# A graph and expert layer on one core: set-up transfers by lane, small loads on GpSimd, and a later wait for DRAM copies

## The chip, the cores and the metric

The kernel runs on one core of a Trainium2 chip. The metric is the device time of one execution in microseconds (us), taken as the median of the runs; lower is better. Engines are named by their work: TensorE (PE), VectorE (DVE), ScalarE (ACT), GpSimd (POOL), and SyncE (SP), which does no arithmetic and whose queue issues DMA transfers. ACT and POOL have DMA queues of their own.

## The reference

One layer over 6250 nodes with 256 features and 200,000 edges sorted by their destination. What matters of it:

```python
edge_index = jnp.stack([src, dst])
xn = _layernorm(x, axis=-1)
x = x + _L0_gnn_ref(xn, edge_index, W, att_src, att_dst, bias) + _L0_mix_ref(xn[None], Wqkv, bqkv, Wproj, bproj, temperature)[0]
x = x + _L0_ffn_ref(_layernorm(x, axis=-1)[None], gate_w, gate_b, w1, b1, w2, b2, gamma, beta)[0]
```

The graph part gathers a projected row for each edge's source, weighs it by a softmax over the edges of its destination, and sums by destination. The mix part is an attention whose keys and values are first summed over all nodes. The last part sends each node to two of 16 experts.

## The kernel before

The work is cut into stages, each a block with a program per engine. At the end of a block all engines meet, and none starts the next block before the last has come. The stages are set-up, projection (50 tiles of 128 nodes), gather (the edges), routing, experts, and the final norm.

Edges are taken in chunks of 496 (CHUNK); 403 chunks are full and one holds the rest of 112. The gather stage wants, for each chunk, a list of source numbers that lies lane by lane: `src_lists` in DRAM is 128 lanes by 408 chunks by 4 places. Lanes 0 to 119 hold four edges of a chunk, lanes 120 to 127 two, and their other places must hold a harmless number. The lists are written by DMA from `src`, DRAM to DRAM. The lists of the first 384 chunks are written beside the tiles of the projection stage, eight chunks at a time (lines 871 and 873); the tail, chunks 384 to 403, is written in set-up.

In set-up the SP queue issues, in this order: the first destinations and the padded destinations, the node features x into `resid` (lines 343 and 345), the pads of `src_lists` (line 348, and line 351 once for each of eight lanes), the tail of the lists for lanes 0 to 119 (line 354), a wait for the pads, the tail for lanes 120 to 127 (line 357), the last chunk (line 359), six tiles of zero rows (line 362), eight loads of one temperature each into `t_col` (line 366) and one of `bq_col` (line 367), `b1_cols` (line 369), and four tiles of `dst_bc` (line 372). It then waits until all DRAM copies but the pads have landed (`scratch_out`). VectorE meanwhile takes the statistics of x, and near its end waits for the small loads (line 484) before it scales `t_col` (line 485) and turns `meet`. GpSimd issues three bias loads (line 389) and, once VectorE has computed where each block of nodes begins, four gathers of destination rows, `d_rows` (line 394).

At the head of the projection stage VectorE clears the last 32 lanes of `rows_g` (line 751), clears four PSUM banks (line 753) and sets constants; ScalarE's first copy of `p_row` (line 643) waits for the last of them. At the end of that stage SP waits for the lists written beside the tiles and fetches the first ones for the gather stage.

Of the kernel before, what the change touches and what calls it, by code (L numbers as in the profile page):

```python
# [19 lines left out]
P = 128  # L20
# [117 lines left out]
def gps_layer(nc, x, src, dst, gnn_W, att_src, att_dst, gnn_bias, Wqkv, bqkv, Wproj, bproj, temperature,  # L138
# [12 lines left out]
    with top:  # L151
# [57 lines left out]
        rows_g = sb("rows_g", [P, R, TC, ROW], ctx=early)  # L209
        idx_in = [sem(f"idx_in{i}", early) for i in range(2)]  # L210
        gather_opened = sem("gather_opened", early)
        gathered = [sem(f"gathered{i}", early) for i in range(R)]

        def gather(pool, q, j):
# [29 lines left out]
        with ExitStack() as c:  # L244
# [50 lines left out]
            x_rest_in = sem("x_rest_in", c)  # L295
            w_in = sem("w_in", c)
            b_in = sem("b_in", c)
            t_in = sem("t_in", c)
            att_zeroed = sem("att_zeroed", c)
            att_in = sem("att_in", c)  # L300
            pads_set = sem("pads_set", c)
            scratch_out = sem("scratch_out", c)
            lists_padded = sem("lists_padded", c)
            ident_ready = sem("ident_ready", c)
            turned = sem("turned", c)
            copied = sem("copied", c)
# [18 lines left out]
            @block.sync  # L325
            def _(sp):
                full = E // CHUNK
                rest = E - full * CHUNK
                even = full - full % 16
                for lo, hi in ((0, even), (even, full)):  # L330
                    sp.dma_start(fd[:, lo:hi], dst[lo * CHUNK:hi * CHUNK].rearrange("(c b) -> c b", b=CHUNK)[:, 0:1].rearrange("c a -> a c"),
                                 allow_slow_non_contiguous=True).then_inc(first_in, 16)
                sp.dma_start(fd[:, full:full + 1], dst[full * CHUNK:full * CHUNK + 1].unsqueeze(0)).then_inc(first_in, 16)
                for lo, hi in ((0, even), (even, full)):
                    sp.dma_start(dst_pad[lo:hi, :], dst[lo * CHUNK:hi * CHUNK].rearrange("(a b) -> a b", b=CHUNK)).then_inc(dst_padded, 16)
                sp.dma_start(dst_pad[full:full + 1, 0:rest], dst[full * CHUNK:E].unsqueeze(0)).then_inc(dst_padded, 16)
                sp.wait_ge(pads_set, 3)
                sp.dma_start(dst_pad[full:full + 1, rest:CHUNK], pad_i[0:1, 0:CHUNK - rest]).then_inc(dst_padded, 16)
                sp.dma_start(dst_pad[full + 1:CHUNKS, :], pad_i[0:CHUNKS - full - 1, :]).then_inc(dst_padded, 16)
                sp.wait_ge(x_zeroed, 1)  # L340
                for q in range(4):
                    n = NFULL // 4
                    sp.dma_start(resid[:, q * n:(q + 1) * n, :],
                                 x[q * n * P:(q + 1) * n * P, :].rearrange("(t p) f -> p t f", p=P)).then_inc(x_in[q], 16)
                sp.dma_start(resid[0:NREST, NFULL, :], x[NFULL * P:N, :]).then_inc(x_rest_in, 16)
                u4 = TILES_PER_CHUNK
                last = rest // u4
                sp.dma_start(src_lists[:, full:CHUNKS, :], pad_s[:, 0:(CHUNKS - full) * u4].rearrange("p (a u) -> p a u", u=u4)).then_inc(lists_padded, 16)
                lo = LIST_TILES * LIST_CHUNKS
                for p in range(LANES, P):  # L350
                    sp.dma_start(src_lists[p:p + 1, 0:full, :].rearrange("p a u -> p (a u)").rearrange("p (a b) -> (p a) b", a=u4),
                                 pad_s[0:u4, 0:full]).then_inc(lists_padded, 16)
                tail = src[lo * CHUNK:full * CHUNK].rearrange("(a b) -> a b", b=CHUNK)
                sp.dma_start(src_lists[0:LANES, lo:full, :].rearrange("p a u -> a p u"),
                             tail[:, 0:BASE].rearrange("a (p u) -> a p u", u=u4)).then_inc(scratch_out, 16)
                sp.wait_ge(lists_padded, (1 + EXTRA) * 16)
                sp.dma_start(src_lists[LANES:P, lo:full, 0:FULL_TILES].rearrange("p a u -> a p u"),
                             tail[:, BASE:CHUNK].rearrange("a (p u) -> a p u", u=FULL_TILES)).then_inc(scratch_out, 16)
                sp.dma_start(src_lists[0:last, full:full + 1, :].rearrange("p a u -> p (a u)"),
                             src[full * CHUNK:E].rearrange("(p u) -> p u", u=u4)).then_inc(scratch_out, 16)  # L360
                for t in range(T, TQ):
                    sp.dma_start(xn_turned[t * P:(t + 1) * P, :], zrow[:]).then_inc(scratch_out, 16)
                heads = temperature.rearrange("a h b c -> (a h b c)")
                for h in range(H):
                    p0 = (h % HALF) * C
                    sp.dma_start(t_col[p0:p0 + C, h // HALF:h // HALF + 1], heads[h:h + 1].unsqueeze(0).broadcast_to([C, 1])).then_inc(t_in, 16)
                sp.dma_start(bq_col[:], bqkv[0:D].rearrange("(g p) -> p g", p=P), allow_slow_non_contiguous=True).then_inc(t_in, 16)
                sp.wait_ge(copied, len(turns) + 1)
                sp.dma_start(b1_cols.rearrange("e p c -> p e c"), b1_t[:].rearrange("p (e c) -> p e c", e=NEXP)).then_inc(scratch_out, 16)
                for g in range(G4):  # L370
                    sp.wait_ge(rows_taken, g + 1)
                    sp.dma_start(dst_bc[g * P:(g + 1) * P, :], d_bf[g][:]).then_inc(scratch_out, 16)
                sp.wait_ge(scratch_out, (3 + TQ - T + G4 + 1) * 16)

            @block.gpsimd
            def _(pool):
# [11 lines left out]
                for ap, vec, n in ((b_kv, bqkv[D:3 * D], 2 * D), (b_proj, bproj, D), (b_gnn, gnn_bias, D)):  # L388
                    pool.dma_start(ap[:], bcast_rows(vec, n)).then_inc(b_in, 16)
                pool.iota(ci[:], [[1, CHUNKS]], base=0, channel_multiplier=0).then_inc(chunk_nr, 1)  # L390
                pool.wait_ge(dst_padded, 5 * 16)
                pool.wait_ge(b_ready, 1)
                for g in range(G4):
# [3 lines left out]
            def _(dve):  # L397
# [82 lines left out]
                dve.reciprocal(rstd[:], rstd[:])  # L480
                dve.drain()
                dve.scalar_tensor_tensor(out=nmr[:], in0=mv[:, :, 0], scalar=-1.0, in1=rstd[:], op0=ALU.mult, op1=ALU.mult)
                dve.wait_ge(b_in, 3 * 16)
                dve.wait_ge(t_in, (H + 1) * 16)
                dve.tensor_scalar(t_col[:], t_col[:], SCALE * SCALE, None, ALU.mult)
                dve.wait_ge(meet_turned, 1)
                dve.tensor_copy(meet[:, 0:FCH, :], p_meet[:, 0:FCH * C].rearrange("p (m i) -> p m i", i=C))
# [77 lines left out]
        with ExitStack() as c:  # L565
# [182 lines left out]
            @block.vector  # L748
            def _(dve):
                dve.memset(zeros[:], 0.0)  # L750
                dve.memset(rows_g[P - C:P].rearrange("p r u f -> p (r u f)"), 0.0)
                for bank in p_main + p_tg:
                    z = dve.memset(bank[:], 0.0)
                z.then_inc(zeroed, 1)
                dve.tensor_scalar(vmask[:], valid[:], 1.0 / N, None, ALU.mult)
                for s in range(2):
                    dve.memset(k1[s][:], 1.0)
# [103 lines left out]
            def _(sp):  # L861
# [15 lines left out]
                for t in range(LIST_TILES, T):  # L877
                    body(t, t % 2)
                sp.wait_ge(lists_out, 2 * LIST_TILES * 16)
                fetch_lists(sp, 0, 0)  # L880
                fetch_lists(sp, R, 1)
                for s in range(2):
# [1149 lines left out]
```

## Time and profile before

| | us |
|---|---|
| median of 3 runs | 3235.82 |
| the runs | 3235.3, 3235.82, 3238.56 |
| the profiled execution | 3240.07 |
| its span | 3238.3 |
| set-up, in the profile | 0 to 78.3 |
| first to last gather of the gather stage | 403.7 to 2478.2 |

The profile is one execution. Its times count from the start of the span; a row of the timeline gives the start, the duration, the engine, the line of the kernel, what is written and read, and in brackets how long the engine was idle before and what released it. SPq, ACTq and POOLq are the queues that issue DMAs: the duration of such a row is that of the issue, not of the transfer. PEclk is the granted clock of TensorE, 1.00 for 2.4 GHz.

### The profile page before, as it was taken

What the parts mean: (1) busy time and instruction counts of PE and PEld (TensorE: products, weight loads), DVE (VectorE), ACT (ScalarE), POOL (GpSimd) and SP (SyncE); (2) the same over time, 40 slices, a digit from 0 to 9 for tenths busy, and PEclk for the clock granted to TensorE, in tenths of its full rate; (3) what the DMA queues carried; (4) which work ended last, traced back from release to release, by engine and by line L of the source; (5) the groups of instructions that cost most, each with busy time, mean ns of one, the idle gap of its engine ahead of it and who ended that gap; (6) DMA issues with size and microseconds to landing.
All of it is one profiled execution on the core that took longest, in us unless ns stands there. A gap on an engine that the chain in (4) does not pass through costs nothing. (4 is left out here: it accounts for less than half of the span.)

```text
span 3238.3 us, 54302 instructions
## 1 busy us (share of the span) xinstructions
PE 2620.3 (81%) x12344; PEld 1709.4 (53%) x12344; DVE 2165.1 (67%) x5140; ACT 1459.4 (45%) x3473; POOL 2079.2 (64%) x2145
## 2 busy tenths in 40 slices
PE   2999978888887888888787888888755438999996
PEld 1455444444544455454444454554444437888884
DVE  5888877767777676777777676777767844333335
ACT  1444465545555555555464555555433221222226
POOL 0577777777777777777777777777775572222224
PEclk9999989989999898999899989889986559999998
DMA  5222244444545444454444444444443156777867
GB/s 146 44 46 45 41 141 136 141 137 130 142 130 142 131 139 134 136 142 130 142 131 136 136 136 136 136 134 132 134 132 90 58 183 188 232 233 233 233 203 244
DMA packets 303697, 454.51 MB, mean 140 GB/s; under 512 B 121983, under 2 KB 198072, under 8 KB 303442
## 3 DMA queue, kind: packets, MB, share of 16 engines
q0 software_dynamic: 88848, 243.01, 26.7%
q1 hardware_dynamic: 186434, 135.90, 15.7%
q10 hardware_dynamic: 28176, 72.95, 6.9%
q8 instruction: 84, 1.38, 0.2%
q14 instruction: 155, 1.27, 0.1%
HBM read 396.32 MB, written 56.94 MB: 140 GB/s over the span
## 5 line engine op out<-in xcount | busy, mean ns | idle before, releaser
L219 POOL DMA_INDIRECT rows_g<-node_rows,idx x1616 | 1577.9, 976 | 497.8 <-issue 461.1
L1211 PE MATMUL p_m<-msg,sel 128*128 128x264 f32 x3616 | 1043.6, 438 | 254.3 <-DVE msg L1179 207.7
L1211 PEld LDWEIGHTS p_m<-msg,sel 128*128 128x128 f32 x3616 | 727.3, 212 | 390.6 <-issue 272.0
L1179 DVE TENSOR_TENSOR msg<-rows_g,p_w 128x1024 f32<-128x1024 f32 x452 | 550.6, 1218 | 44.8 <-ACT p_w L1077 43.7
L1077 ACT ACTIVATE p_w<-lg 128x32 f32<-128x32 f32 x452 | 91.0, 201 | 785.1 <-DVE lg L1172 783.8
L1863 POOL DMA_INDIRECT moe<-ysb,token x128 | 124.0, 969 | 366.3 <-DVE ysb L1852 343.3
L1168 DVE TENSOR_TENSOR lg<-rows_g,ends 128x32 f32<-128x32 f32 x452 | 87.2, 193 | 406.7 <-SPq L1011 306.0
L1032 ACT ACTIVATE sel_t<-apart,ones 128x512 bf16<-128x512 bf16 x455 | 328.4, 722 | 32.1 <-issue 0.7
L1101 DVE TENSOR_TENSOR sel<-p_w,dst_t 128x512 f32<-128x512 f32 x453 | 312.1, 689 | 26.4 <-issue 9.3
L1029 ACT ACTIVATE apart<-dst_all,iota_neg 128x512 bf16<-128x512 bf16 x455 | 321.6, 707 | 0.0
L1201 PEld LDWEIGHTS p_sp<-adm_parts,sel_t 128*128 128x128 bf16 x1816 | 94.5, 99 | 382.1 <-issue 374.2
L1055 ACT ACTIVATE qfeat<-p_scr 128x512 f32<-128x512 f32 x442 | 239.4, 588 | 116.9 <-PE p_scr L1234 111.2
L1818 ACT ACTIVATE ht<-e_ph,ba 128x256 f32<-128x256 f32 x256 | 100.3, 474 | 418.2 <-PE e_ph L1788 418.2
L562 POOL TENSOR_TENSOR acc<-kk 128x512 f32<-128x512 f32 x150 | 167.7, 1147 | 156.5 <-DVE kk L796 156.5
L1234 PE MATMUL p_scr<-q_t,sel_sum 32*128 32x512 f32 x832 | 248.8, 653 | 5.2 <-DVE q_gram L1130 5.2
L1788 PE MATMUL e_ph<-xst,wa 128*128 128x256 f32 x1024 | 233.3, 382 | 4.2 <-DMA bb<-in_L_ffn_b_dram 2.5
L1797 PE MATMUL e_py<-wb,ht 128*128 128x256 f32 x1024 | 231.5, 380 | 0.0
L1788 PEld LDWEIGHTS e_ph<-xst,wa 128*128 128x128 f32 x1024 | 195.7, 192 | 31.8 <-issue 5.5
L1201 PE MATMUL p_sp<-adm_parts,sel_t 128*128 x1816 | 125.1, 188 | 107.5 <-DVE lg L1172 97.7
L1827 DVE COPY xst<-e_px 128x512 f32<-128x512 f32 x64 | 44.3, 692 | 238.1 <-PE e_px L1778 238.1
L1797 PEld LDWEIGHTS e_py<-wb,ht 128*128 128x128 f32 x1024 | 190.1, 191 | 22.8
L1110 DVE TENSOR_TENSOR acc<-acc,p_m 128x264 f32 x452 | 194.1, 430 | 6.1 <-PE p_m L1211 3.5
(331 smaller groups left out, 3358.1 us busy)
## 6 DMA issues: line engine op xcount, KB each, us to landing
dst_all<-dst_bc ACTq DMA_DIRECT2D x115, 512.0 KB, 4.2
wa<-in_L_ffn_w_dram SPq DMA_DIRECT2D x64, 512.0 KB, 4.8
wb<-in_L_ffn_w_dram SPq DMA_DIRECT2D x64, 512.0 KB, 5.3
rows_g<-node_rows,idx POOLq DMA_INDIRECT x1616
xs<-slot_x SPq DMA_DIRECT2D x64, 258.0 KB, 2.9
ya<-moe SPq DMA_DIRECT2D x48, 256.0 KB, 4.4
bb<-in_L_ffn_b_dram SPq DMA_DIRECT2D x64, 128.0 KB, 5.6
qs<-xn_turned ACTq DMA_DIRECT2D x13, 512.0 KB
```

The costliest lines, as they stand in the source:

```text
L219: pool.indirect_dma_start(rows_g[0:n, j, u, :], None, node_rows, bass.IndirectOffsetOnAxis(ap=idx[q][0:n, j, u:u + 1], axis=0)).then_inc(g ...
L1029: act.activation(apart[j % 2][:], dst_all[q][:, j, :], ACT.Square, bias=iota_neg[:])
L1032: act.activation(sel_t[j][:], apart[j % 2][:], ACT.Relu, bias=ones[:, 0:1], scale=-1.0).then_inc(sel_t_ready, 1)
L1055: act.activation(feat[slot(name)][:], bank(name)[:], ACT.Square).then_inc(act_freed, 1)
L1101: dve.tensor_tensor(sel[j][:], p_w[:, P:2 * P].unsqueeze(1).broadcast_to([P, TC, P]), d.unsqueeze(2).broadcast_to([P, TC, P]), ALU.is_equa ...
L1110: dve.tensor_tensor(a, a, p_m[j % 2][:, 0:ROW], ALU.add).then_inc(acc_added, 1)
L1179: dve.tensor_tensor(m4, g3[:, :, 0:D].rearrange("p u (h e) -> p u h e", h=H), p_w[:, 0:TC * H].rearrange("p (u h) -> p u h", u=TC).unsquee ...
L1201: mm = pe.matmul(p_e(j)[:, u * 6 * H:(u + 1) * 6 * H], sel_t[j][:, u * P:(u + 1) * P], adm_parts[:, bass.ds(b, 1), :, :].rearrange("p a r ...
L1211: mm = pe.matmul(p_m[j % 2][:, 0:ROW], sel[j][:, u, :], msg[j % 2][:, u, :], start=(u == 0), stop=(u == TC - 1))
L1234: pe.matmul(bank(name)[:], sel_sum[rows, m * P:(m + 1) * P], q_t[g][rows, :], start=True, stop=True).then_inc(act_filled, 1)
L1788: mm = pe.matmul(p_h[s % 2][:, m * SLOT_ROWS:(m + 1) * SLOT_ROWS], wa[s][:, k, m * P:(m + 1) * P], xst[s % 2][:, k, :], start=(k == 0), st ...
L1797: mm = pe.matmul(p_y[s % 2][:, a * D:(a + 1) * D], ht[s % 2][:, k, a * P:(a + 1) * P], wb[s][:, k, :], start=(k == 0), stop=(k == KF - 1))
```

## The change

Five edits, all of set-up and of its two neighbours in time:

- The eight pad transfers, one per spare lane, become four that each cover all eight lanes.
- The tail of the lists is described lane first (`p a u`) on both sides, in place of chunk first (`a p u`). The bytes are the same.
- The eight loads of `t_col` and the load of `bq_col` move from SP's queue to GpSimd's, behind the bias loads, and count on the same semaphore `b_in`.
- The three tail transfers count on a new semaphore, `tail_out`. SP waits for it at the end of the projection stage, before the first lists are fetched, and no longer at the end of set-up.
- The fill of `rows_g` moves behind the PSUM fills and covers only the places that a partial gather leaves open (two of four).

```diff
-                for p in range(LANES, P):
-                    sp.dma_start(src_lists[p:p + 1, 0:full, :].rearrange("p a u -> p (a u)").rearrange("p (a b) -> (p a) b", a=u4),
-                                 pad_s[0:u4, 0:full]).then_inc(lists_padded, 16)
+                spare_lanes = src_lists[LANES:P, 0:full, :].rearrange("p a u -> p (a u)")
+                for q in range(u4):
+                    sp.dma_start(spare_lanes[:, q * full:(q + 1) * full], pad_s[0:EXTRA, 0:full]).then_inc(lists_padded, 16)
                 tail = src[lo * CHUNK:full * CHUNK].rearrange("(a b) -> a b", b=CHUNK)
-                sp.dma_start(src_lists[0:LANES, lo:full, :].rearrange("p a u -> a p u"),
-                             tail[:, 0:BASE].rearrange("a (p u) -> a p u", u=u4)).then_inc(scratch_out, 16)
-                sp.wait_ge(lists_padded, (1 + EXTRA) * 16)
-                sp.dma_start(src_lists[LANES:P, lo:full, 0:FULL_TILES].rearrange("p a u -> a p u"),
-                             tail[:, BASE:CHUNK].rearrange("a (p u) -> a p u", u=FULL_TILES)).then_inc(scratch_out, 16)
+                sp.dma_start(src_lists[0:LANES, lo:full, :], tail[:, 0:BASE].rearrange("a (p u) -> p a u", u=u4)).then_inc(tail_out, 16)
+                sp.wait_ge(lists_padded, (1 + u4) * 16)
+                sp.dma_start(src_lists[LANES:P, lo:full, 0:FULL_TILES], tail[:, BASE:CHUNK].rearrange("a (p u) -> p a u", u=FULL_TILES)).then_inc(tail_out, 16)
                 sp.dma_start(src_lists[0:last, full:full + 1, :].rearrange("p a u -> p (a u)"),
-                             src[full * CHUNK:E].rearrange("(p u) -> p u", u=u4)).then_inc(scratch_out, 16)
+                             src[full * CHUNK:E].rearrange("(p u) -> p u", u=u4)).then_inc(tail_out, 16)
...
-                heads = temperature.rearrange("a h b c -> (a h b c)")
-                for h in range(H):
-                    p0 = (h % HALF) * C
-                    sp.dma_start(t_col[p0:p0 + C, h // HALF:h // HALF + 1], heads[h:h + 1].unsqueeze(0).broadcast_to([C, 1])).then_inc(t_in, 16)
-                sp.dma_start(bq_col[:], bqkv[0:D].rearrange("(g p) -> p g", p=P), allow_slow_non_contiguous=True).then_inc(t_in, 16)
...
-                sp.wait_ge(scratch_out, (3 + TQ - T + G4 + 1) * 16)
+                sp.wait_ge(scratch_out, (TQ - T + G4 + 1) * 16)
...
+                heads = temperature.rearrange("a h b c -> (a h b c)")
+                for h in range(H):
+                    p0 = (h % HALF) * C
+                    pool.dma_start(t_col[p0:p0 + C, h // HALF:h // HALF + 1], heads[h:h + 1].unsqueeze(0).broadcast_to([C, 1])).then_inc(b_in, 16)
+                pool.dma_start(bq_col[:], bqkv[0:D].rearrange("(g p) -> p g", p=P), allow_slow_non_contiguous=True).then_inc(b_in, 16)
...
-                dve.wait_ge(b_in, 3 * 16)
-                dve.wait_ge(t_in, (H + 1) * 16)
+                dve.wait_ge(b_in, (3 + H + 1) * 16)
...
-                dve.memset(rows_g[P - C:P].rearrange("p r u f -> p (r u f)"), 0.0)
                 for bank in p_main + p_tg:
                     z = dve.memset(bank[:], 0.0)
                 z.then_inc(zeroed, 1)
+                dve.memset(rows_g[P - C:P, :, FULL_TILES:, :], 0.0)
...
                 sp.wait_ge(lists_out, 2 * LIST_TILES * 16)
+                sp.wait_ge(tail_out, 3 * 16)
                 fetch_lists(sp, 0, 0)
```

## Rows read from the trace of the kernel before

**Rows 1.** Timeline of SP's queue in set-up: start, issue time, line, transfer, count.

```profile
30.63 2.90 SPq L351 DMA_DIRECT2D src_lists<-pad_s  x8
33.58 0.75 SPq L354 DMA_DIRECT2D src_lists<-in_src_dram  x1
38.53 23.14 SPq L357 DMA_DIRECT2D src_lists<-in_src_dram  x1
61.72 1.73 SPq L359 DMA_DIRECT2D src_lists<-in_src_dram  x1
63.49 2.97 SPq L362 DMA_DIRECT2D xn_turned<-zrow  x6
66.50 3.70 SPq L366 DMA_DIRECT2D t_col<-n_L_mix_temperature_dram  x8
70.25 0.43 SPq L367 DMA_DIRECT2D bq_col<-in_L_mix_bqkv_dram  x1
70.73 0.46 SPq L369 DMA_DIRECT2D b_cols<-b_t  x1
71.23 2.43 SPq L372 DMA_DIRECT2D dst_bc<-d_bf  x4
```

**Rows 2.** Waits of SP's queue: for what, us in total, times, longest.

```profile
SPq L244 <- DMA dst_bc<-d_bf: 4.2, 1, 4.2
```

**Rows 3.** Timeline of VectorE's and ScalarE's rows at set-up's end.

```profile
45.33 0.21 DVE L482 SCALAR_TENSOR_TENSOR nmr<-mv,rstd 128x50 f32<-128x50 f32 x1
...
72.51 0.17 DVE L485 TENSOR_SCALAR t_col<-t_col 128x2 f32<-128x2 f32 x1 [26.97 <-DMA bq_col<-in_L_mix_bqkv_dram]
...
73.06 0.17 DVE L489 TENSOR_SCALAR meet<-meet 32x32 f32<-32x32 f32 x1
78.28 1.09 ACT L630 ACTIVATE xn<-resid,nmr,rstd 128x256 f32<-128x256 f32 x2 [33.53 <-PEq L244]
```

**Rows 4.** Windows: length, busy PE, PEld, DVE, ACT, POOL, PEclk, DMA share, GB/s.

```profile
44.00:50.00 6.00, 0.00 (x0) 0.00 (x0) 1.08 (x5) 0.24 (x1) 0.00 (x0) 1.00 0.12 1
...
66.00:68.00 2.00, 0.00 (x0) 0.00 (x0) 0.00 (x0) 0.00 (x0) 0.00 (x0) 1.00 0.63 202
...
72.00:74.00 2.00, 0.00 (x0) 0.00 (x0) 0.63 (x3) 0.00 (x0) 0.00 (x0) 1.00 1.08 103
```

**Rows 5.** One line's instructions: count, duration min/median/max in ns, first and last start.

```profile
L871 SPq DMA_DIRECT2D src_lists<-in_src_dram x48: 702/754/826, 88.6 to 382.7; - x48
```

**Rows 6.** Timeline of GpSimd in set-up, and VectorE's last use of d_rows.

```profile
3.69 0.56 POOL L389 DMA_DIRECT2D b_gnn<-in_L_gnn_bias_dram  x1
...
22.98 1.02 POOL L394 DMA_INDIRECT d_rows<-dst_pad,cidx  x1 [18.29 <-DVE b L451]
...
33.34 0.63 DVE L471 TENSOR_SCALAR d_bf<-d_rows,b 128x480 bf16<-128x480 int32 x1
```

**Rows 7.** Timeline of the projection stage: VectorE's fill, and TensorE after gaps.

```profile
79.84 3.58 DVE L751 MEMSET rows_g<- 32x4224 f32 x1 [0.92 <-issue]
...
89.25 1.46 PE L711 MATMUL p_row<-w_cat,xt 128*128 128x272 f32 x4 [4.52 <-ACT xt L637]
...
90.50 3.35 PE L711 MATMUL p_kv<-w_cat,xt 128*128 128x512 f32 x4
...
378.32 1.88 PE L711 MATMUL p_kv<-w_cat,xt 128*128 128x512 f32 x4
...
398.60 1.92 PE L684 MATMUL p_main<-acc,vm 128*32 128x512 f32 x16 [2.52 <-DVE acc L562]
```

**Rows 8.** Windows of the projection stage: TensorE alone, then all engines.

```profile
91.00:92.00 1.00, 1.00 (x2) 0.50 0.25 71
...
320.00:340.00 20.00, 19.90 (x112) 11.02 (x111) 17.33 (x42) 10.14 (x33) 14.59 (x17) 1.00 0.24 49
```

**Rows 9.** The gathers of line 219: durations in ns, and what ended idle time.

```profile
L219 POOL DMA_INDIRECT rows_g<-node_rows,idx x1616: 947/987/1487, 403.7 to 2478.2; - x180
...
  DVE msg L1179: 33.3, 101
```

More of the change, by code:

```diff
@@ L211, in gps_layer @@
         gather_opened = sem("gather_opened", early)
+        tail_out = sem("tail_out", early)
         gathered = [sem(f"gathered{i}", early) for i in range(R)]
@@ L297, in gps_layer @@
             b_in = sem("b_in", c)
-            t_in = sem("t_in", c)
             att_zeroed = sem("att_zeroed", c)
@@ L301, in gps_layer @@
             pads_set = sem("pads_set", c)
+            lists_padded = sem("lists_padded", c)
             scratch_out = sem("scratch_out", c)
-            lists_padded = sem("lists_padded", c)
             ident_ready = sem("ident_ready", c)
```

## The prediction

> **What bounds the kernel now.** I read the profile from the edit outwards. The slices of the page show two long stages that the change does not enter: the gather stage, and the expert stage behind it. In the gather stage GpSimd issues 1616 gathers in 2074.5 us, one each 1.28 us: 0.99 for the issue itself and 0.3 to the next one. Only 33.3 us of it is a wait for VectorE [rows 9]. Its length is set by the number of gathers, so a gain in set-up moves this stage forward and does not shorten it.
>
> The change lies in set-up (0 to 78.3 us) and at the head of the projection stage. The timeline of the SP queue shows that one issue, line 357, holds the queue from 38.53 to 61.67 [rows 1]. The windows show why: from 44 to 50 us the DMA engines are at a share of 0.12 and move 1 GB/s [rows 4]; this is the first of five windows that are alike, up to 64 us. The transfer of line 354, issued at 33.58, has 19 chunks as its outermost count and 19 x 120 = 2280 pieces of 16 bytes; it crawls on a corner of the DMA engines, and the next issue waits until its pieces are through. Everything behind it is late: eight loads of t_col and the load of bq_col are issued at 66.50 and 70.25, and VectorE, ready at 45.54, waits for them 26.97 us [rows 1, 3]. ScalarE sits from 44.8 until the next block opens at 78.28 [rows 3]. Yet VectorE's own last step ends at 73.23; what closes the block is SP, which issues dst_bc until 73.66 and waits 4.2 us for the landing, to 77.87 [rows 1 to 3]. The barrier takes the other 0.4.
>
> **The change part by part.**
>
> Pads (line 351). Eight issues of 2.90 us in all [rows 1] become four: 1.45 less at the front. It buys nothing alone, because SP then stands until 38.53 for the landing of the pads (the wait ahead of line 357) [rows 1], which lie behind the x loads. I keep 38.53. Bounds: 36.5 if the landing follows fewer pieces and the queue behind x (at 36 to 38 us almost nothing moved), 40.4 if the new tail, now on the same engines as all pads, costs them its own 1.9 us (next part).
>
> Tail of the lists (lines 354, 357, 359). Now lane by lane: outermost count 120, with the same pieces read from src. One corner of the engines took from about 34 to 64 us for some 2400 pieces, 12.4 ns a piece; spread over 15 to 16 engines that is 1.9 us. The nearest row of a spread transfer is b1_cols: 2048 pieces of 16 bytes with 128 outermost, gone together with the first of dst_bc in the windows 72 to 74, where the share is 1.08 [rows 4]. The lists of the later tiles, 960 pieces with 8 outermost, are issued in a median of 754 ns and never hold SP [rows 5]. So line 357 costs 0.75 in place of 23.14 and line 359 0.75 in place of 1.73 [rows 1, 5]; bounds 0.3 each (a pad's issue) and 1.7. The Trainium skill, "DMA: Bandwidth & Descriptors", section on why a DMA increments its semaphore by 16, says that a transfer runs on the largest number of engines up to 16 that divides the outermost counts of both sides: by it 19 gives one engine and 120 gives fifteen. No row here shows a transfer with 120 outermost.
>
> Small loads. The nine leave SP, 3.70 + 0.43 us with the steps between them 4.2 [rows 1], and go to GpSimd behind its iota, at 4.69. GpSimd's own loads take 0.56 each in the last case [rows 6] and up to 0.74; nine are 5.0 to 6.6 us, so it is free by about 11.5. It waits there for VectorE until 22.98 [rows 6], a cover of 11 us. If the cover were gone, the four gathers of d_rows behind them would start late; the last is used at 33.34 without slack [rows 6], and VectorE would slip by as much. VectorE's one merged wait for b_in at 45.5 finds all landed. Here a page speaks against the edit. The Trainium skill, "SBUF — State Buffer", on the trap that VectorE blocks DMAs issued from GpSimd, says that these descriptors can't be written while a VectorE instruction in a two-port mode runs. The trace does not bear it out at this place: GpSimd issued b_gnn in 0.56 us at 3.69 to 4.25, beside VectorE's back-to-back fills [rows 6].
>
> New end of the block. SP: 38.53, then 0.75 + 0.75 for lines 357 and 359, 2.97 for the zero rows, 0.46 for b1_cols, 2.43 for dst_bc, and five steps of 0.05: 46.1 [rows 1]. The landing of dst_bc takes 4.2 more [rows 2]. The 768 KB of zero rows ran at about 200 GB/s [rows 4], some 1.3 us past their own issue; in the kernel before, the nine loads gave them time to drain, now b1_cols follows at once. I add 1.0 (bounds 0 and 1.3), which makes 51.3, and the barrier of 0.4: the next block opens at 51.7, against 78.28. Gain 26.6. The next to be late is VectorE: 45.54 and its last three steps of 0.75, done at 46.3, 5.0 us under SP. The wait for tail_out now stands before the first list fetch, at about 365 us; it costs nothing, its transfers are long down, and what is queued behind it on SP (the list fetches) loses nothing.
>
> Bounds of this term: earliest 51.7 - 2.0 (pads) - 0.9 (two issues) - 1.0 (backlog) = 47.8; latest 51.7 + 1.9 + 1.9 + 0.3 = 55.8. The gain is 22.5 to 30.5.
>
> Fill of rows_g. In the projection stage VectorE fills 4224 columns in 3.58 us [rows 7] before the PSUM fills and the constants that ScalarE's first copy waits for. It now fills 2112 after the PSUM fills: at the same rate 1.79, so 1.79 less on that path; the first tile was waiting for it, since TensorE's first projection was done by 84.5. Gain 1.8, with no cover.
>
> TensorE's clock. In this gap TensorE idled 4.52 us before 89.25 [rows 7], its granted clock then fell to 0.50 (1.2 of 2.4 GHz) [rows 8], and the four matmuls of p_kv took 3.35 us [rows 7] against 1.88 in a later tile [rows 7]. With the fill shortened the gap is 4.52 - 1.79 = 2.73. A gap of 2.52 us later in the stage kept the upper level: the sixteen matmuls behind it ran in the usual 1.92 [rows 7]. 2.73 is nearer to that than to 4.52, so I take the clock as kept: 3.35 - 1.88, gain 1.5. The bounds are 0 and 1.5. From there the stage is full of TensorE (19.90 of 20 us [rows 8]), so an early first tile stays early.
>
> **The sum.** 26.6 + 1.8 + 1.5 = 29.9 us. The profiled execution took 3240.07 (span 3238.3), so its like would be 3210.2; the median of the three runs is 4.25 lower, and I apply the same difference: 3235.82 - 29.9 = 3205.9.
>
> **The rivals.**
>
> A: the tail does not spread (0.06). If the pieces still go through one corner, line 357 stalls for its 23.14 again. Then only the nine loads leave SP, 4.2, plus 1.8: 3235.8 - 6.0 = 3229.8. For it: the bytes and the pieces are the same. Against it: the lists with 8 outermost and b1_cols with 128 both run without a stall [rows 4, 5].
>
> B: another cover is used up (0.06). Either reading 16-byte pieces at a stride of a chunk costs some five times the 12.4 ns, so that 152 pieces per engine last 9.4 us in place of 1.9 and hold zero rows, b1_cols and dst_bc, all on the same engines (7.5 later); or the small loads take over 1.9 us each on GpSimd and push d_rows and VectorE past the 5.0 us of room. Priced by the first: 3213.4. Speaking for it: 16-byte reads at a stride are seen in no row. Against: the writes of before were scattered in the same way at 12.4 ns. The skill's rule on the shared port takes the second road: if not one of the nine loads got through before VectorE's b128 was ready at 22.1, they would end near 28, d_rows would be 5.0 late and VectorE level with SP. By the issue times of this trace that is 3205.9 still; it decides only from there on, and 0.01 of B's chance is for it.
>
> C: slower (0.03). In the gather stage VectorE holds GpSimd 101 times, 33.3 us in all [rows 9]; VectorE stands there behind TensorE, whose clock moves between 0.78 and 1.00 from one 50 us window to the next. An earlier start deals these phases anew. The hold would have to grow from 33.3 to over 63 us for the result to be worse than before; at 70 it would be 3242. For it: the profiled run was 4.25 over the median of the others. Against it: three runs lay within 3.3 us, so a growth of 30 is far out of what this stage does by itself.
>
> **How the numbers follow.** The main case has 0.85; its own range is gains from 22.5 + 1.8 + 0 - 2 (spread of runs) = 22.3 to 30.5 + 1.8 + 1.5 + 2 = 35.8, that is 3200.0 to 3213.5. B's price is just inside; this is the range for 8 in 10. A measurement of this kernel can tell about 0.2% (6.5 us) from no change. Faster by more: the main case and B, 0.91. Within: A, whose 6.0 is just under, 0.06. Slower: C, 0.03.
>
> **What would show it.** Line 357's issue under 2 us and zero rows issued from about 40; the DMA share of 0.12 gone; VectorE's wait for t_col gone and its last step of set-up near 46.3; the next block open at 47.8 to 55.8 with SP's wait for dst_bc as the last one; the first copy of p_row 1.8 us sooner after the opening; the second tile's four matmuls of p_kv in 1.9 (kept) or 3.35 (lost); the gather stage, first to last gather, at 2074.5 us as before within 2. A stalled line 357 would make A true, and d_rows used later than 33.3 would point to B. The forecast is wrong if the first gather does not move by about 30 from 403.65, or if the later stages give part of it back.

## The result, and the profile after

| | before | changed |
|---|---|---|
| median, first set of runs, us | 3235.61 (3235.3 to 3238.56, 4 runs) | 3211.41 (3209.23 to 3213.59, 4 runs) |
| ratio, with its 95% interval | | 0.9923 (0.9911 to 0.9934) |
| median, second set | 3237.72 (3234.68 to 3240.88, 9 runs) | 3217.47 (3210.66 to 3219.61, 5 runs) |
| ratio, second set | | 0.9936 (0.9922 to 0.9949) |
| the profiled execution | 3240.07 | 3213.59 |
| next block opens after set-up | 78.28 | 54.51 |
| first gather | 403.7 | 376.3 |

The change is faster by 24.2 us in the first set and by 20.3 in the second. The forecast was 3205.9, a gain of 29.9, with a range from 3200.0 to 3213.5: the first median lies inside, 5.5 above the forecast. The second, 3217.47, lies 4.0 above the end of the range, and its gain of 20.3 is below the smallest gain of the range, 22.3.

SP's queue in the changed kernel, by its timeline (start, issue time, line, transfer, count), answers to [rows 1]:

```profile
31.36 2.06 SPq L352 DMA_DIRECT2D src_lists<-pad_s  x4
33.47 0.97 SPq L354 DMA_DIRECT2D src_lists<-in_src_dram  x1
42.59 0.73 SPq L356 DMA_DIRECT2D src_lists<-in_src_dram  x1
43.36 0.85 SPq L357 DMA_DIRECT2D src_lists<-in_src_dram  x1
44.25 2.96 SPq L360 DMA_DIRECT2D xn_turned<-zrow  x6
47.25 0.45 SPq L362 DMA_DIRECT2D b_cols<-b_t  x1
47.75 2.49 SPq L365 DMA_DIRECT2D dst_bc<-d_bf  x4
```

The stall of 23.14 us is gone: the second tail transfer (now line 356) is issued in 0.73. But it starts at 42.59 and not at 38.53. SP's waits, which answer to [rows 2], name the reason:

```profile
SPq L356 <- DMA src_lists<-pad_s: 8.1, 1, 8.1
SPq L245 <- DMA dst_bc<-d_bf: 3.8, 1, 3.8
```

The rest of set-up, by the timeline of GpSimd, VectorE and ScalarE [rows 3, 6]:

```profile
4.64 4.02 POOL L387 DMA_DIRECT2D t_col<-n_L_mix_temperature_dram  x8
...
8.65 0.75 POOL L388 DMA_DIRECT2D bq_col<-in_L_mix_bqkv_dram  x1
...
23.01 1.04 POOL L392 DMA_INDIRECT d_rows<-dst_pad,cidx  x1 [13.61 <-DVE b L449]
...
45.48 0.16 DVE L482 TENSOR_SCALAR t_col<-t_col 128x2 f32<-128x2 f32 x1
...
46.02 0.17 DVE L486 TENSOR_SCALAR meet<-meet 32x32 f32<-32x32 f32 x1
...
54.51 1.09 ACT L627 ACTIVATE xn<-resid,nmr,rstd 128x256 f32<-128x256 f32 x2 [9.74 <-PEq L245]
```

VectorE's idle time ahead of t_col is gone, the small loads are off GpSimd by 9.40, and SP alone closes the block. The head of the projection stage answers to [rows 7]:

```profile
57.86 1.82 DVE L751 MEMSET rows_g<- 32x2112 f32 x1 [0.49 <-issue]
...
58.29 3.43 PE L708 MATMUL p_kv<-w_cat,xt 128*128 128x512 f32 x4
...
61.82 0.38 ACT L640 COPY row<-p_row 128x264 f32<-128x264 f32 x1 [5.55 <-PE p_kv L708]
...
63.29 1.18 PE L708 MATMUL p_row<-w_cat,xt 128*128 128x272 f32 x4 [1.35 <-ACT xt L634]
...
64.31 1.88 PE L708 MATMUL p_kv<-w_cat,xt 128*128 128x512 f32 x4
```

And the gathers, which answer to [rows 9]:

```profile
L220 POOL DMA_INDIRECT rows_g<-node_rows,idx x1616: 952/987/1507, 376.3 to 2453.2; - x180
...
  DVE msg L1177: 31.1, 94
```

### The profile page after: what moved, and what is told of

The parts are those of the page before. It is cut to its first block and busy times, and to the rows that moved or that the text cites. A ratio compares the mean times of both kernels' runs of the same rounds, so it can differ in the third digit from the quotient of the medians.

```text
span 3211.8 us, 54298 instructions
## 1 busy us (share of the span) xinstructions
PE 2620.5 (82%) x12344; PEld 1708.0 (53%) x12344; DVE 2164.7 (67%) x5140; ACT 1460.0 (45%) x3473; POOL 2085.8 (65%) x2154
## 5 line engine op out<-in xcount | busy, mean ns | idle before, releaser
L1027 ACT ACTIVATE apart<-dst_all,iota_neg 128x512 bf16<-128x512 bf16 x455 | 321.7, 707 | 0.0
```

Of the source, the lines that this page charges most:

```text
L1027: act.activation(apart[j % 2][:], dst_all[q][:, j, :], ACT.Square, bias=iota_neg[:])
```

## The experiments

The theory after the result: the gain is the end of the stall of line 357, and what is missing of it was lost at the wait for the pads, which the tail, now spread over the engines right behind them, holds up (theory T). Its rival is that the four wide pad transfers land late by themselves (P). Of the tail's slowness there are two accounts, strided reads (S) and any spread small pieces (Q); of TensorE, theory K ties its clock to the gap that the fill shortens. The labels in brackets are those that the expectations use. Twelve runs were made, of ten kernels besides the changed one, which ran again, as did best1; u_ kernels undo a part of the changed kernel, o_ kernels make one part alone in the kernel before. Most have one profiled execution beside one of the kernel before, so they are read by places in the trace and not by their time: single executions took 3209.6 us (u_pads) to 3218.7 (iso) where the tail is spread, 3233.0 with the small loads only and 3231.8 with the fill only, beside 3237.7 to 3241.7 for the kernel before. A table of the places comes at the end of this section.

### The tail behind the pads' wait (u_order)

```diff
-                sp.dma_start(src_lists[0:LANES, lo:full, :], tail[:, 0:BASE].rearrange("a (p u) -> p a u", u=u4)).then_inc(tail_out, 16)
                 sp.wait_ge(lists_padded, (1 + u4) * 16)
+                sp.dma_start(src_lists[0:LANES, lo:full, :], tail[:, 0:BASE].rearrange("a (p u) -> p a u", u=u4)).then_inc(tail_out, 16)
```

> The changed kernel, but the big tail transfer (lane first, 2280 pieces) is issued behind the wait for the pads and not ahead of it. Theory T (the tail, spread over the engines and issued right behind the pads, holds up the pads' landing, which took SP to 42.59 us): the wait for the pads ends at 38.5 or before, and the tail, now alone on the engines, shows its own length in the DMA windows. Rival P (the four wide pad transfers land late by themselves): the wait still ends near 42.6. If the tail's pieces cost 12.4 ns each on one engine and spread over 15, its stretch is 2 us long; if a read at a stride costs five times as much, 8 us.

SP's queue by the timeline:

```profile
38.41 0.96 SPq L355 DMA_DIRECT2D src_lists<-in_src_dram  x1
...
45.12 10.61 SPq L365 DMA_DIRECT2D dst_bc<-d_bf  x4
```

The wait ended at 38.41: theory T holds and P falls. The gain was not kept: the four issues of dst_bc took 10.61 us in place of 2.49, one of them alone 9.1, and the next block opened at 57.70, 3.2 us later than in the changed kernel. The spread tail costs whoever is queued around it, the pads ahead of it or dst_bc behind it.

### The narrow pads back (u_pads)

```diff
-                spare_lanes = src_lists[LANES:P, 0:full, :].rearrange("p a u -> p (a u)")
-                for q in range(u4):
-                    sp.dma_start(spare_lanes[:, q * full:(q + 1) * full], pad_s[0:EXTRA, 0:full]).then_inc(lists_padded, 16)
+                for p in range(LANES, P):
+                    sp.dma_start(src_lists[p:p + 1, 0:full, :].rearrange("p a u -> p (a u)").rearrange("p (a b) -> (p a) b", a=u4),
+                                 pad_s[0:u4, 0:full]).then_inc(lists_padded, 16)
...
-                sp.wait_ge(lists_padded, (1 + u4) * 16)
+                sp.wait_ge(lists_padded, (1 + EXTRA) * 16)
```

> The changed kernel with the eight narrow pad transfers of before in place of the four wide ones. Theory T: the wait for the pads still ends near 42.6. Rival P: it ends near 38.5 as before the change, and the next block opens 4 us sooner than 54.5.

The wait ended at 43.03 and the block opened at 55.00. With eight narrow transfers the landing is as late as with four wide ones, so the pads' form is not the cause. The opening is 0.5 us later than the changed kernel's, no more than two profiles of that kernel differ (54.51 and 55.04), so no gain of the pads' edit by itself is shown.

### The tail only (o_tail)

The two transfers of chunks 384 to 402 lane first in the kernel before, awaited in set-up as before, and nothing else.

> The kernel before with one part alone: the three tail transfers lane first (awaited in set-up as before, narrow pads, small loads on SP). If the corner of the engines was all of the stall: the issue of line 357 under 1 us, but the pads' wait ends near 42.6 by theory T (38.5 by P), then zero rows, nine loads (4.2 us), b1_cols, dst_bc; the next block opens near 78.3 - 22 + 4 = 58 to 60 by T, 54 to 56 by P. It would be worth some 18 to 20 of the 26.5 us that the profiled runs differ.

The second tail transfer on SP's queue, and ScalarE's first instruction of the next block:

```profile
44.74 0.72 SPq L356 DMA_DIRECT2D src_lists<-in_src_dram  x1
...
60.77 1.09 ACT L628 ACTIVATE xn<-resid,nmr,rstd 128x256 f32<-128x256 f32 x2 [16.00 <-PEq L244]
```

The block opened at 60.77, 17.5 us sooner than 78.28, with the wait for the pads ending at 44.74. This is by far the largest part of the gain; the opening is a little later than the 58 to 60 of T. The small loads alone give 3.6 (below), so the two parts together account for 21.1 of the 23.8 us by which the changed kernel opens sooner; of the other 2.7, 2.2 is the end of the pads' wait, 44.74 against 42.59, a place that differs by 1.4 between two profiles of the changed kernel itself. Here set-up still waited for the tail, and its last wait was put down to dst_bc, 3.8 us, as in the changed kernel: keeping the tail's wait in set-up cost nothing to be seen in this kernel.

### The tail by itself (iso)

All else of set-up first, then the big tail transfer with nothing beside it, then a wait for it alone:

```diff
-                sp.dma_start(src_lists[0:LANES, lo:full, :], tail[:, 0:BASE].rearrange("a (p u) -> p a u", u=u4)).then_inc(tail_out, 16)
...
                 sp.wait_ge(scratch_out, (TQ - T + G4 + 1) * 16)
+                sp.dma_start(src_lists[0:LANES, lo:full, :], tail[:, 0:BASE].rearrange("a (p u) -> p a u", u=u4)).then_inc(tail_out, 16)
+                sp.wait_ge(tail_out, 16)
...
```

The two small tail transfers stand behind that wait.

> The price in dispute by itself: the changed kernel with the big tail transfer (lane first) issued when everything else of set-up has landed, and SP waiting for it alone before it issues the two small ones and closes the block. Without the tail in the way the wait for the pads ends by 38.5 and dst_bc has landed near 48. Then issue to landing of the tail: 12.4 ns a piece on each of fifteen engines gives 1.9 us and some 2 us of landing, 4 in all; theory S (a read of 16 bytes at a stride of a chunk costs about 50 ns) gives 8 and 2, 10 in all.

SP's queue and its wait, then the windows (length, PEclk, DMA share, GB/s), the last two of them finer:

```profile
48.53 0.96 SPq L363 DMA_DIRECT2D src_lists<-in_src_dram  x1
60.42 0.73 SPq L365 DMA_DIRECT2D src_lists<-in_src_dram  x1
```

```profile
SPq L365 <- DMA src_lists<-in_src_dram: 10.9, 1, 10.9
```

```profile
48.00:50.00 2.00, 1.00 0.00 0
50.00:52.00 2.00, 1.00 0.46 13
52.00:54.00 2.00, 1.00 0.14 4
54.00:56.00 2.00, 1.00 0.04 1
56.00:58.00 2.00, 1.00 0.00 0
58.00:60.00 2.00, 1.00 0.00 0
...
54.25:54.50 0.25, 1.00 0.14 4
54.50:54.75 0.25, 1.00 0.00 0
```

From the start of the issue to the landing it takes 11.9 us. I had put 1.9 for the pieces and about 2 for landing. The first pieces show 1.7 us after the start of the issue, and the last are through by 54.5, some 4 us later, most of them in the first two; then for 5.9 us no transfer is recorded and the semaphore still does not come. The shares of the windows add up to 20.5 us of one engine's time (0.64 of 16 engines over 2 us), 9 ns for each of the 2280 pieces. This is an estimate. It is below 12.4, and below the 24 ns that the same reckoning gives for the confined pieces (0.12 of 16 engines over 30 us for some 2400): the price of a piece was not put too low. What the 1.9 us lacked is the time around the pieces. Theory S, a steady 8 us of slow pieces, is not seen either, although its total of 10 is the nearer one. Spread out, the tail went from some 28 us (an estimate: 2280 pieces at 12.4 ns) to 11.9, not to a fifteenth.

### The tail chunk first, in 16 and 3 chunks (split)

```diff
-                sp.dma_start(src_lists[0:LANES, lo:full, :], tail[:, 0:BASE].rearrange("a (p u) -> p a u", u=u4)).then_inc(tail_out, 16)
+                lists_t, chunks_t = src_lists[0:LANES].rearrange("p a u -> a p u"), tail[:, 0:BASE].rearrange("a (p u) -> a p u", u=u4)
+                for a0, a1 in ((0, 16), (16, full - lo)):
+                    sp.dma_start(lists_t[lo + a0:lo + a1], chunks_t[a0:a1]).then_inc(tail_out, 16)
...
-                sp.wait_ge(tail_out, 3 * 16)
+                sp.wait_ge(tail_out, 4 * 16)
```

> The changed kernel with the big tail chunk first as before, but in two transfers of 16 and 3 chunks: 16 and 3 are the outermost counts, the reads are whole rows of 1920 bytes, the writes 16 bytes each. Theory S (the strided reads are what is slow and holds up the pads): the wait for the pads ends near 39 and the next block opens near 51. Rival Q (any tail that is spread over the engines right behind the pads holds them up, by its scattered pieces): the wait still ends near 42.6. If the outermost count were not what spreads a transfer, line 357's stall of 23 us would be back.

The timeline shows the two issues together (line 356) and the end of the wait (line 358):

```profile
33.87 4.11 SPq L356 DMA_DIRECT2D src_lists<-in_src_dram  x2
41.95 0.72 SPq L358 DMA_DIRECT2D src_lists<-in_src_dram  x1
```

The stall of 23 us did not come back: the same chunk-first pieces, with 16 and 3 outermost in place of 19, flow, though the longer of the two issues took 3.42 us. That shows the outermost count to be what confined the transfer of before. The wait ended at 41.95, far from S's 39: whole-row reads did not free the pads, so the strided read is not what holds them up. Rival Q, that any spread tail right behind them does, is the nearer one. The block opened at 53.04.

### SP's queue turned round (best1, best1_r, and after_r beside it)

Zero rows, b1_cols and dst_bc first; the wait for the pads and the three tail transfers behind them:

```diff
-                sp.dma_start(src_lists[0:LANES, lo:full, :], tail[:, 0:BASE].rearrange("a (p u) -> p a u", u=u4)).then_inc(tail_out, 16)
-                sp.wait_ge(lists_padded, (1 + u4) * 16)
-                sp.dma_start(src_lists[LANES:P, lo:full, 0:FULL_TILES], tail[:, BASE:CHUNK].rearrange("a (p u) -> p a u", u=FULL_TILES)).then_inc(tail_out, 16)
-                sp.dma_start(src_lists[0:last, full:full + 1, :].rearrange("p a u -> p (a u)"),
-                             src[full * CHUNK:E].rearrange("(p u) -> p u", u=u4)).then_inc(tail_out, 16)
                 for t in range(T, TQ):
...
                     sp.dma_start(dst_bc[g * P:(g + 1) * P, :], d_bf[g][:]).then_inc(scratch_out, 16)
+                sp.wait_ge(lists_padded, (1 + u4) * 16)
+                sp.dma_start(src_lists[0:LANES, lo:full, :], tail[:, 0:BASE].rearrange("a (p u) -> p a u", u=u4)).then_inc(tail_out, 16)
+                sp.dma_start(src_lists[LANES:P, lo:full, 0:FULL_TILES], tail[:, BASE:CHUNK].rearrange("a (p u) -> p a u", u=FULL_TILES)).then_inc(tail_out, 16)
+                sp.dma_start(src_lists[0:last, full:full + 1, :].rearrange("p a u -> p (a u)"),
+                             src[full * CHUNK:E].rearrange("(p u) -> p u", u=u4)).then_inc(tail_out, 16)
                 sp.wait_ge(scratch_out, (TQ - T + G4 + 1) * 16)
```

> The changed kernel with the order of SP's queue turned round: zero rows, b1_cols and dst_bc ahead of the wait for the pads, all three tail transfers behind it; the block still closes on the landing of dst_bc and the rest. SP issues dst_bc from 37.4 to 39.9, it lands by 44 to 45, so VectorE's 46.3 closes the block and the next opens near 46.7, 7.8 us sooner than 54.5. If the tail, issued at about 40, slows dst_bc's landing, it opens at 50. The first copy of p_row then still waits for TensorE, 7.3 us after the opening, and the first gather comes near 368.5.

The block opened at 46.47 as expected, with VectorE as the last to come. The first gather came at 369.9 and not at 368.5, since TensorE's clock was lost once more (below), and the span ended at 3212.0, level with the changed kernel's 3211.8. Both kernels were timed again together:

> The changed kernel again, timed beside best1_r on one chip. If the gather stage's length (2071 to 2082 us in ten profiles, all of it in the length of the single issues) is a matter of the run, the gains of the set-up will show in the medians: about 3211. If it belongs to the kernel, this one keeps a gather stage of about 2077.

> The kernel of best1 again, with rounds. Its profile opened the projection stage 8.0 us sooner than the changed kernel and began the gathers 6.4 us sooner, but ended at the same time: 4.4 us went in the gather stage, 2.2 behind it. If that is chance (issues of 980 ns against 978 on average, over 1616), the median is 3205 to 3206, some 5 to 6 us under after_r. If an earlier start makes the gather stage longer, it is level with after_r within 2 us and its profile again has 2081 us from first to last gather.

The changed kernel's median was 3217.47, as in the table above. The turned-round one had 3206.74 (3203.02 to 3208.39, 4 runs), 0.9904 of the kernel before (0.9889 to 0.9919): 31.0 us faster than before and 10.7 faster than the changed kernel beside it. The runs of the two do not overlap, so the turned-round kernel is faster. Both expectations missed in size: the changed kernel was put at about 3211 and the difference at 5 to 6. The profiles show 8.4 us of the 10.7, at the opening and again at the first gather; where the rest lies they do not show, as each is of the fastest run of its kernel, and these two differ by 7.6. The loss of the clock in the first profile did not come again in the second. In that one the block opens at 46.67 and the first gather comes at 368.3:

```profile
34.00 2.79 SPq L355 DMA_DIRECT2D xn_turned<-zrow  x6
36.84 0.46 SPq L357 DMA_DIRECT2D b_cols<-b_t  x1
37.34 4.81 SPq L360 DMA_DIRECT2D dst_bc<-d_bf  x4
42.19 0.97 SPq L362 DMA_DIRECT2D src_lists<-in_src_dram  x1
```

The tail is now behind all that set-up waits for, and its landing falls into the projection stage. This kernel beats both the one before and the changed one.

### The same, with the big tail transfer still ahead (best2)

> As best1, but the big tail transfer stays right behind the pads, ahead of the zero rows. If its pieces share the rings with dst_bc (u_order: issue of dst_bc 10.6 us), b1_cols and dst_bc are slow and the block opens at 50 to 54; if only the waiting for the pads had mattered, it opens near 47 as best1.

Its issues ran into the tail: the zero rows took 6.5 us to issue in place of 2.8, dst_bc 9.2, and the block opened at 51.64. So it is not the wait for the pads alone that costs; the transfer itself must be behind dst_bc. Not all of the long issue is the tail's: in the first turned-round profile, with no tail ahead, one issue of dst_bc took 3.8 us, and here one took 7.8.

### The small loads only (o_loads)

> The kernel before with one part alone: the nine small loads on GpSimd's queue. Line 357 still holds SP for some 23 us. By the sum the next block opens 4.2 us sooner, at 74.1, and the first copy of p_row is 9.4 us behind it as before; if the loads had only given the zero rows time to drain, half a microsecond to one of that is lost again in the landing of dst_bc. GpSimd is free by 11.5 and d_rows is issued at 23.0 as before.

The block opened at 74.70: 3.6 us sooner, against 4.2 of the sum, and the wait for the pads ended 0.6 later than before (39.13). VectorE had nothing to wait for. d_rows was unharmed, as in the changed kernel.

### The fill of rows_g: undone, and alone (u_fill, o_fill)

```diff
+                dve.memset(rows_g[P - C:P].rearrange("p r u f -> p (r u f)"), 0.0)
                 for bank in p_main + p_tg:
                     z = dve.memset(bank[:], 0.0)
                 z.then_inc(zeroed, 1)
-                dve.memset(rows_g[P - C:P, :, FULL_TILES:, :], 0.0)
```

> The changed kernel with the fill of rows_g as before: all 4224 columns, ahead of the PSUM fills. Set-up unchanged: the block opens at 54.5. Theory K (the shorter gap of TensorE keeps its clock): the first copy of p_row comes 9.4 us after the opening in place of 7.3; TensorE idles some 3.5 us or more between the first two tiles, its clock is lost, and the second tile's four matmuls of p_kv take 3.4 us in place of 1.9; the first gather comes 3.6 to 3.9 us later than 376.3. Rival (the clock is not tied to this gap): 2.1 us later only, with p_kv at 1.9.

> The kernel before with one part alone: the fill of rows_g halved and behind the PSUM fills. The block opens at 78.3 as before. The first copy of p_row comes 2.1 to 2.3 us sooner after it. Theory K: TensorE's gap between the first two tiles falls from 4.5 to some 2.3 us, the clock stays, the second tile's four matmuls of p_kv take 1.9 in place of 3.35, and the first gather comes 3.7 to 4.0 us sooner than 403.65. If a gap of this length can still lose the clock (best1's of 2.09 did), it comes 2.2 us sooner only.

TensorE's timeline at the second tile, first with the fill undone, then with the fill alone changed in the kernel before:

```profile
67.05 2.18 PE L708 MATMUL p_row<-w_cat,xt 128*128 128x272 f32 x4 [3.92 <-ACT xt L634]
69.02 3.59 PE L708 MATMUL p_kv<-w_cat,xt 128*128 128x512 f32 x4
```

```profile
86.74 1.18 PE L711 MATMUL p_row<-w_cat,xt 128*128 128x272 f32 x4 [2.54 <-ACT xt L637]
87.76 1.88 PE L711 MATMUL p_kv<-w_cat,xt 128*128 128x512 f32 x4
```

With the fill undone the gap is 3.92 us, both groups of matmuls of the second tile run at the lower clock, and the first gather comes 326.4 us after the opening in place of 321.8. That is 4.6 and not the 3.6 to 3.9 expected, 1.0 of it because p_row too ran at the lower clock (2.18 against 1.18). With the fill alone the gap is 2.54, the clock stays, and it comes 321.7 after the opening in place of 325.4. What theory K expected came true in both directions; that the length of the gap alone does not decide is said below.

### All profiles side by side

"Opens" is the start of ScalarE's first instruction of the projection stage; p_kv is the time of the four matmuls of the second tile; all in us.

| kernel | pads' wait ends | opens | TensorE's gap | p_kv | opening to first gather | first to last gather |
|---|---|---|---|---|---|---|
| before | 38.53 | 78.28 | 4.52 | 3.35 | 325.4 | 2074.5 |
| changed | 42.59 | 54.51 | 1.35 | 1.88 | 321.8 | 2076.9 |
| changed, again | 43.97 | 55.04 | 1.33 | 1.88 | 321.7 | 2075.0 |
| tail behind the wait | 38.41 | 57.70 | 1.34 | 1.88 | 321.8 | 2076.8 |
| narrow pads back | 43.03 | 55.00 | 1.33 | 1.88 | 321.9 | 2074.5 |
| tail only | 44.74 | 60.77 | 3.92 | 3.59 | 326.4 | 2070.9 |
| tail by itself | 38.63 | 62.78 | 2.44 | 1.88 | 321.5 | 2075.8 |
| chunk first, 16 and 3 | 41.95 | 53.04 | 1.22 | 1.88 | 322.0 | 2081.6 |
| turned round | | 46.47 | 2.09 | 2.62 | 323.4 | 2081.3 |
| turned round, again | | 46.67 | 2.43 | 1.88 | 321.6 | 2077.1 |
| turned round, tail ahead | | 51.64 | 2.25 | 1.88 | 321.8 | 2081.5 |
| small loads only | 39.13 | 74.70 | 4.63 | 3.13 | 325.4 | 2074.8 |
| fill undone | 43.45 | 56.07 | 3.92 | 3.59 | 326.4 | 2073.7 |
| fill only | 38.43 | 77.97 | 2.54 | 1.88 | 321.7 | 2073.7 |

## Why the prediction was right, point by point

**The stall of line 357.** Right. It was the tail's transfer, confined by its outermost count, and it went: line 356 in 0.73 us against 0.75 in the sum, line 357 in 0.85. The experiment with 16 and 3 chunks shows the count as the cause, apart from the layout; the tail alone gave 17.5 us. Rival A (not spread) is out.

**The tail's own length.** This term was mis-sized, and it is the main error. I put 1.9 us and it took 11.9 from issue to landing. The step that failed was to let the pieces stand for the whole transfer. Their price was not too low (9 ns of engine time each where the tail runs alone, by the estimate above), but they were spread over some 4 us and not 1.9, began 1.7 after the issue, and the semaphore came 5.9 after the last of them; the sum had nothing for these. The rival B had the right sort of event in mind (7.5 us longer) but the wrong victim behind it: dst_bc was held by nothing in the changed kernel (its wait was 3.8 us, less than the 4.2 before), because SP had already lost the time at the pads. With the tail behind the pads' wait or ahead of the zero rows dst_bc was held, by issues of 9.1 and 7.8 us.

**The pads' wait.** I kept 38.53 and gave 40.4 as the later bound. It ended at 42.59 and 43.97 in two profiles, outside the bound. The bound was made of the tail's 1.9 us and so inherited the first error. The zero rows were issued from 44.25 and not from about 40. The four issues of the pads took 2.06 us and not 1.45; SP's wait behind them covered that. That the tail is what delays the wait is shown (38.41 with the tail behind it).

**The end of the block.** Forecast 51.7, bounds 47.8 to 55.8, measured 54.51. The difference of 2.8 is the pads' 4.1 less 1.4 at the landing of dst_bc, where I had added 1.0 of backlog to 4.2 and which took 3.8, and 0.1 of small steps. SP closed the block and VectorE was done at 46.2, as the sum had it (46.3).

**The small loads.** Right: off GpSimd at 9.40 (forecast: by 11.5), d_rows issued at 23.01 and used at the same time as before. The eight loads of t_col took 0.50 us each beside VectorE's casts, and bq_col 0.75 with VectorE's fill of 4.23 us beginning at 8.74. The rule of the Trainium skill, "SBUF — State Buffer", section "SBUF: two separate sides", on descriptors held up by VectorE is not to be seen in these issues; whether one of VectorE's instructions beside them ran in such a mode, the trace does not tell. What did change is the landing: a load of t_col landed 7.3 us after its issue (median; 1.7 on SP's queue in the kernel before) and bq_col 8.4 after (2.2). Loads of att_bd on ScalarE's queue at that time took as long (medians of 8.5 and 8.7), so the traces do not put it down to GpSimd. All had landed by 17.1, long before VectorE's wait at 45.5.

**The fill.** 1.8 forecast, 2.1 in the changed kernel and 2.2 alone (9.40 to 7.20 from the opening to the first copy). In the changed kernel the copy was released by TensorE's p_kv, done at 61.72, and no longer by VectorE, done at 61.68: the prediction saw no such cover, and a still shorter fill would have gained next to nothing there. The fill itself went from 3.58 to 1.82; the missing 0.4 is the pause ahead of it, 0.92 before and 0.49 now.

**TensorE's clock.** Kept, as forecast, 3.35 to 1.88, and with the fill worth 3.6 us together (325.4 to 321.8) against 3.3 forecast. The gap was 1.35 and not 2.73, as TensorE finished its first projection later (p_kv in 3.43 against 2.45 in the kernel before). Why is not shown: the granted clock is recorded at 1.00 over the first tile in both, while the 3.43 is the pace of the lower clock. So the gap that the forecast rested on was not the one that came. Taking the clock's fate from the gap's length alone was too simple: 2.09 us lost it in one profile of the turned-round kernel, while 2.25, 2.43, 2.44 and 2.54 kept it in others. Nor did the fall come at one place of the gap. With the fill undone the granted clock fell some 2.5 us into the idle time (65 to 66 us at 0.81). In the kernel before it stayed at 1.00 through all of the 4.52 us and fell 0.8 after the matmuls had begun again. Why it falls at one place and not at another is not shown. The granted clock in the kernel before, then in the profile with 2.09 (length, busy PE, PEclk, DMA share, GB/s):

```profile
85.00:89.00 4.00, 0.00 (x0) 1.00 0.01 2
89.00:90.00 1.00, 0.75 (x3) 1.00 0.39 135
90.00:91.00 1.00, 1.00 (x3) 0.51 0.43 13
```

```profile
55.00:56.00 1.00, 0.75 (x2) 0.64 0.39 135
56.00:57.00 1.00, 1.00 (x4) 0.50 0.43 13
57.00:58.00 1.00, 1.00 (x2) 0.50 0.32 77
```

**The later stages.** "Its length is set by the number of gathers" holds only to 0.5%: in fourteen profiles it lay between 2070.9 and 2081.6 us, and in the changed kernel it was 2.4 longer, just beyond the 2 that I had allowed. Rival C looked for this in VectorE's hold on GpSimd; the hold was 27 to 34 us throughout and did not move with it. What moved was the issue itself, 974 to 981 ns on average, times 1616. A later opening went loosely with a shorter stage in the first ten profiles, but the second profile of the turned-round kernel, which opens earliest but for its first, had 2077.1; no rule is shown. In the profiled pair, of 27.4 us gained at the first gather 25.0 were left at the last and 26.5 at the end. The prediction's own last sign, a first gather that moves by about 30 and later stages that give nothing back, came only in part: 27.4 moved and 0.9 went back.

**The median.** I carried over the difference of 4.25 us between profiled run and median. It was 2.2 in the first set and the other way round in the second, where the profiled run was the lowest of five. The miss of 5.5 is 2.8 from the opening, 0.9 from the later stages and 2.1 from this conversion, less 0.3 that the fill gave beyond its forecast. That the median lies inside the range is in part luck: in the second set the same kernel lies outside it. Of the 6.1 us between its two medians 2.1 is found in the kernel before too (3235.61 and 3237.72); the rest no trace shows.

**Rival A's price.** It leaves out the clock, although the fill was changed in its case too. With the 1.5 of the sum its gain is 7.5 and its time 3228.3, which is past the 6.5 us that can be told from no change; its 0.06 should then have gone with the faster cases. The fill alone gave 3.7 us from the opening to the first gather, clock and all.

**Still open.** Why a transfer that is issued before another lands later because of it, and what the tail does between its last recorded piece and its semaphore. No trace here shows the writes' own end. The new place of the tail's wait alone was not tried; the kernel with the tail only, which kept it in set-up, speaks for no gain.

## What to carry to other kernels

When one DMA issue on a queue takes tens of microseconds, look at the transfer ahead of it and at its outermost count, and then at who stands behind it; repairing the count moved 17.5 us here. After the repair, ask where the transfer stands in the queue: what the stage's end needs goes first, and scattered small pieces that are wanted only later go last, which gave 10.7 us more than the change itself, 8.4 of it seen in the traces. Take the price of a transfer from issue to landing in a place where it stands alone; a rate per piece prices the pieces only, and here they were a small part of the 11.9 us.

## What the runs showed of the hardware that I had not expected

- A DRAM to DRAM transfer of 2280 pieces of 16 bytes took 11.9 us from issue to landing with nothing beside it, although its pieces were recorded within some 4 us; the same pieces confined took some 28, by an estimate from 12.4 ns a piece.
- A transfer queued behind others delays their landing: the pads' wait ended at 41.95 to 44.74 with the spread tail behind them, in six profiles, and at 38.41 to 39.13 in the five where the tail was confined or issued later.
- TensorE's clock was lost after an idle gap of 2.09 us and kept after one of 2.54, in like surroundings. In the first tile of the changed kernel four matmuls of p_kv took 3.43 us with the granted clock recorded at 1.00; later ones took 1.88.
- The length of an indirect gather's issue on GpSimd, 974 to 981 ns on average, is not the same from profile to profile, and 1616 of them make up to 10.7 us of it.
